# First layer of a two-layer transformer block: VectorE takes two copies from ScalarE in the gelu steps, the rows of maxima are turned ahead of two matmul pairs, and ten filler matmuls become six

## What is computed

```python
xn = _layernorm(x)
x = x + _L0_attn_ref(xn, ...) + _L0_ffn_ref(xn, ...)
xn = _layernorm(x)
x = x + _L1_attn_ref(xn, ...) + _L1_ffn_ref(xn, ...)
```

## Time and profile before

| | |
|---|---|
| median of 3 runs | 1325.0 us |
| lowest and highest | 1321.04 and 1330.04 us |
| the profiled execution's own time | 1330.59 us |
| its span in the profile | 1328.9 us |
| mean granted clock of TensorE | 0.978 |
| first layer | to about 510 us of the span |

### The profile page before, as it was taken

One profiled execution on the slowest core, in us unless ns is written; L12 is line 12 of the kernel. 1 busy time (PEld: TensorE's weight loads), 2 busy tenths in 40 slices (PEclk: granted clock), 3 DMA queues, 4 the chain that ended last, 5 costly groups with the idle time before them and its releaser, 6 DMA issues.

```text
span 1328.9 us, 23542 instructions
## 1 busy us (share of the span) xinstructions
PE 1286.8 (97%) x8338; PEld 773.1 (58%) x8346; DVE 982.7 (74%) x2344; ACT 828.7 (62%) x1235; POOL 744.0 (56%) x889
## 2 busy tenths in 40 slices
PE   8899999999999999999999999999999999999998
PEld 5444445455544445666666666666666666666666
DVE  4666776877776667777777877877877878878775
ACT  2456576666667655666657666666666666656653
POOL 6154465646555445765655655655655665665553
PEclk9889999999999889999999999999999999999999
DMA  6223233424253141111221120020020120010002
GB/s 191 70 75 94 89 99 105 127 91 130 90 165 108 50 142 38 46 41 45 62 66 45 54 74 21 30 74 21 30 74 21 31 74 21 30 50 22 26 30 74
DMA packets 57751, 90.61 MB, mean 68 GB/s; under 512 B 12315, under 2 KB 23616, under 8 KB 57634
## 3 DMA queue, kind: packets, MB, share of 16 engines
q1 hardware_dynamic: 56482, 88.58, 21.4%
q10 hardware_dynamic: 1152, 0.52, 0.1%
HBM read 43.66 MB, written 44.30 MB: 66 GB/s over the span
## 4 chain that ended last, share of the span: by engine, by line
PE 56%; DVE 2%; ACT 2%; POOL 1%; issue 0%; DVEq 0%
PE bank L1674 7%; PE bank_pair L130 6%; PE bank_pair L155 6%; PE bank_pair L1663 4%; PE bank L1663 4%; PE bank L1675 4%; PE bank L1676 4%; PE bank_pair L1664 4%; PE bank_pair L1665 4%; PE bank L1665 4%; PE bank L1664 4%; PE bank_pair L137 1%; DVE bank_pair L165 1%; DVE a_h L1485 1%; DVE a_h L1491 1%; PE bank_pair L1633 1%
## 5 line engine op out<-in xcount | busy, mean ns | idle before, releaser
L1299 POOL TENSOR_TENSOR a_h_lo<-a_h,a_h_hi 128x512 fp32r<-128x512 f32 x256 | 329.8, 1288 | 129.7 <-ACT a_h_hi L1397 125.4
L189 POOL TENSOR_SCALAR_AFFINE_SELECT E<-E 128x256 f32<-128x256 f32 (+1 forms) x384 | 195.5, 512 | 354.0 <-ACT E L1405 199.3
L689 DVE TENSOR_REDUCE mx<-bank_pair 128x2 f32<-128x1024 f32 (+3 forms) x264 | 209.6, 818 | 119.5 <-PE bank_pair L939 118.1
L1485 DVE SCALAR_TENSOR_TENSOR a_h<-a_h,bank_pair 128x512 f32<-128x512 f32 x256 | 175.5, 686 | 122.1 <-ACT a_h L1393 121.4
L1405 ACT ACTIVATE E<-bank_pair 128x1024 f32<-128x1024 f32 (+1 forms) x192 | 169.8, 884 | 116.3 <-PE bank_pair L137 116.3
L165 DVE CUSTOM_DVE_ANT_0 bank_pair<-bank_pair,mask 128x512 f32<-128x512 f32 x496 | 230.3, 516 | 0.0
L1397 ACT ACTIVATE a_h_hi<-a_h 128x512 fp32r<-128x512 f32 x256 | 161.6, 631 | 86.9 <-DVE a_h L1491 86.9
L779 ACT ACTIVATE E<-bank_pair 128x1024 f32<-128x1024 f32 (+1 forms) x192 | 168.4, 878 | 74.2 <-PE bank_pair L137 72.8
L130 PE MATMUL bank_pair<-st 24*128 24x512 f32 (+3 forms) x1024 | 200.2, 390 | 13.4 <-ACT E L779 4.0
L1393 ACT ACTIVATE a_h<-bank_pair 128x512 f32<-128x512 f32 x256 | 152.1, 594 | 73.3 <-PE bank_pair L1665 70.9
L1491 DVE TENSOR_TENSOR a_h<-a_h,bank 128x512 f32<-128x512 f32 x256 | 175.9, 687 | 26.7
(11 more groups left out here) (209 smaller groups left out, 2278.9 us busy)
## 6 DMA issues: line engine op xcount, KB each, us to landing
st<-stack_d SPq DMA_DIRECT2D x256, 96.0 KB
o_d<-O SPq DMA_DIRECT2D x63, 256.0 KB, 2.1
stack_d<-l_q_k_hi SPq DMA_DIRECT2D x56, 256.0 KB, 3.1
stack_d<-l_q_k_lo SPq DMA_DIRECT2D x28, 256.0 KB, 3.4
st<-ms SPq DMA_DIRECT2D x128, 8.0 KB
wst<-wg_in SPq DMA_DIRECT2D x8, 256.0 KB, 3.2
wst<-wu_in SPq DMA_DIRECT2D x8, 256.0 KB, 3.8
wst<-wd_in SPq DMA_DIRECT2D x8, 256.0 KB, 4.4
```

Source lines behind the costliest of these rows:

```text
L189: return nc.gpsimd.affine_select(out=part, in_=part, compare_op=ALU.is_ge, fill=0.0, base=0, pattern=pattern, channel_multiplier=-1)
L689: ins = nc.vector.tensor_reduce(out, pair[:, :, col:col + width(kb)], AX.X, ALU.max)
L1299: nc.gpsimd.tensor_tensor(h_lo[:, q % RH, :], h[:, q % RH, :], h_hi[:, q % RH, :].bitcast(F32), ALU.subtract).then_inc(h_lo_ready, 1)
L1485: nc.vector.scalar_tensor_tensor(hq, hq, 1.0, g_bank[:, :], ALU.add, ALU.mult).then_inc(silu_ready, 1)
```

## The change

In steps with u = 0 that have gelus (b from 0 to 7), and only there: `outputs(g - 1)` and `copy_mrow(g + 1)` move from ScalarE to VectorE, around `add_tile`; `maxima_rows(g + 1)` moves on TensorE from behind `fc(b, 3)` to ahead of `fc(b, 2)`; and the ten fillers of the following step become six.

```diff
-FILLERS = ((2, 2, 2, 2), (10, 2, 2, 0), (2, 2, 4, 3), (2, 2, 2, 3))
+FILLERS = ((2, 2, 2, 2), (6, 2, 2, 0), (2, 2, 4, 3), (2, 2, 2, 3))
...
+            def outputs(g):
+                dve.wait_ge(pv_done, g + 1)
+                if g > 1:
+                    dve.wait_ge(o_out[g % 2], 16 * (g // 2))
+                nc.vector.tensor_copy(O[:, g % 2, :], pv_bank[:, :]).then_inc(O_copied, 1)
+
+            def copy_mrow(g):
+                dve.wait_ge(mT_ready, g + 1)
+                if g > 1:
+                    dve.wait_ge(mrow_in, MAX_LOADS * (g - 1))
+                nc.vector.tensor_copy(ms[:, g % 2, :], bank_of("M", g, 0)[0:MAXIMA, :]).then_inc(mrow_ready, 1)
...
                 if S:
                     negations(g + 1)
+                if u == 0 and ok(b) and in_range(g - 1):
+                    outputs(g - 1)
                 if q is not None:
                     add_tile(q)
+                if u == 0 and ok(b):
+                    copy_mrow(g + 1)
                 if u == 0 and ok(y2) and g < QUADS:
                     statistics(1, y2)
...
-                if in_range(g - 1):
+                if in_range(g - 1) and not (u == 0 and ok(b)):
                     outputs(g - 1)
...
-                if scored(g + 1):
+                if scored(g + 1) and not (u == 0 and ok(b)):
                     copy_mrow(g + 1)
...
                 if u == 0 and ok(b):
+                    maxima_rows(g + 1)
                     fc(b, 2)
                     fc(b, 3)
                 if u == 1 and ok(y2):
                     queries(1, y2)
-                if scored(g + 1):
+                if scored(g + 1) and not (u == 0 and ok(b)):
                     maxima_rows(g + 1)
```

## The result

| | before | changed |
|---|---|---|
| median | 1321.4 us (20 runs) | 1335.5 us (20 runs) |
| lowest, highest | 1318.4, 1330.0 | 1328.4, 1348.0 |
| ratio to before | | 1.0102, interval 1.0084 to 1.0120 |
| profiled execution, span | 1330.6, 1328.9 | 1330.7, 1329.0 |
| mean granted clock of the profiled execution | 0.978 | 0.977 |

What follows compares the result with a forecast made beforehand. Each passage was bound by ScalarE up to the score unit, then by the normalized tiles' chain, starting on VectorE. Path +0.85 and clock +3.2 gave +4.05 us on 1330.6, 1334.6; less 5.6 for the median, 1329 us; range 1318 to 1340.

Steps and rivals of the forecast that it cites:

- rival (a): Every passage from step 9 on loses the clock at step 29's price: +13.1 us, 1338 us; chance 0.17.
- Points 1 to 3: Gelu passages: output copy frees ScalarE 0.60 us, fc 2 and 3 end 0.33 later, maxima copy's leaving saves 0.45.
- Point 5: VectorE ahead of `add_tile`: the output copy, 0.68 us, fits into 1.26 us of idle time and costs nothing.
- Point 6: VectorE behind `add_tile`: the maxima copy takes 0.68 us and makes the statistics, `xn` and transposes 0.63 us late.
- The path terms: Delays and savings in steps 1, 5, 9, 13, 17, 21, 25 and 29, without the clock: together +0.85 us.
- Point 4: TensorE: four fillers, 1.02 us, must go for the 0.45 us and buy nothing beyond; step 1 saves about 1.7.
- Point 7: TensorE ahead of the transposes: 1.64 us more idle time, four more clock falls at 0.8 us, +3.2 us.
- Rival (b): The 8-partition copy takes 0.17 us, `xn` is only 0.12 us late, the clock gains: middle 1321 us; chance 0.25.
- Rival (c): TensorE's order gives ScalarE's gain back, unseen slack takes up the statistics' delay: 0 us, 1325 us; chance 0.08.

Runs made afterwards that it cites:

- the run with the turn alone: Kernel before with only the turn of the maxima (`maxima_rows`) moved ahead of fc 2, ten fillers, both copies on ScalarE: 1322.2 us, ratio 1.0000.

## Why the prediction was right and wrong

The measured 1335.5 us lies in the range (1318 to 1340), and the direction was right. The size was not: +4 us forecast, +14.1 measured, nearer to rival (a), which I gave 0.17. That the time lies inside is in part luck: the range was drawn wide enough to take in rival (a), +13.1 us, and it stood on a median of 1325.0 us from three runs, where twenty give 1321.4. The mechanism was right, a longer wait for the tiles and the clock; the term for the clock was mis-sized by a factor of four, and the fillers' part in it was missing.

- Points 1 to 3, ScalarE: the table load started right behind the exponential, the gelus were bound by TensorE at the back, as said. The gain was 0.58 us rather than 0.45, and as forecast none of it reached the end of the passages 9 to 21. In step 5 all of it did (0.58 for 0.45). Step 1 is shorter, from its first table load to the output copy 16.32 us (48.06 to 64.38) in place of 17.54 (47.27 to 64.81): 1.2 us, where I had 1.7.
- Point 5, the output copy: covered, 0.68 us. Right, and the run with it alone shows no loss clear of noise.
- Point 6, the maxima copy: forecast 0.68 us and 0.63 us of delay; measured 0.68 and 0.64, and 0.60 us a passage in step 9. Right for the passages like it. Two other terms of the sum were off, and cancelled. For steps 13 and 21 I took 0.24 us each, because the tiles had been early there. They were early because the clock was low (0.50 from 226.90 to 230.10 us and from 342.90 to 346.10) and TensorE late; in the run with the turn alone, where the clock was full, it waits 0.40 us in both, and the change costs 0.6. Steps 25 and 29 I read as like step 9, but there TensorE had no idle time ahead of the transposes before the change; step 25 shows 0.18 in place of 0.63. The path terms together come to about +1.0 us, and I had +0.85.
- What the path costs in the times agrees with that only roughly: two runs of the changed kernel and three of the other at the same mean clock of 0.983 differ by some 2.6 us (1328.4 and 1328.5 against 1325.7 to 1326.1). The 1.5 us between the two figures are not settled.
- Point 4 failed in one sentence: that beyond the 0.45 us the removed fillers "buy nothing". Taken out alone they cost 7.4 us. Their worth was the clock, and I counted idle time only for the two edits together, behind the score unit.
- Point 7, the clock, is the mis-sized term. I took four falls at 0.8 us. A fall in these passages costs 3.5 us (20.14 against 16.67). The price of 0.7 us came from setting step 6 against step 10 and taking the wait of 2.10 us off. But step 10 is not step 6 at the full clock. In the profile of the changed kernel with ten fillers step 6 keeps the full clock, through the same wait of 2.10 us, and takes 14.24 us, where it took 18.38:

```profile
125.39:139.63 14.24, 12.10 (x110) 6.37 (x111) 10.30 (x26) 7.93 (x11) 8.01 (x13) 1.00 0.20 69
```

So the loss of the clock costs 4.1 us in step 6 too. Step 29, with 2.45 us, was the nearer row and still low: with the full clock it takes 16.34 us in the run with the turn alone, where it took 18.80. Three falls at 3.5 in place of four at 0.8 make the sum +11.3 us, and a fourth +14.8. The median clocks say the same, as an estimate: 0.975 against 0.989 over 1335 us is 37 us more at half rate (0.014 x 1335 / 0.5), and at 3.5 us for 10 us of it that is 13 us.

- The carry-over from the profiled execution to the median, 5.6 us, was from three runs; with twenty it is 9.2 us. The profiled execution of before had more low clock (0.978) than the median one (0.989 in the runs beside the experiments). Falls counted in its profile, such as in step 29, were no fixed part of the time before, so more of them could be new: that hid a part of the loss.

Rival (b) is out: the copies of 8 and of 128 partitions took 0.68 us each, and the kernel is not faster. Rival (c) is out too.

## What to carry to other kernels

Fillers on TensorE may look surplus where the engine that TensorE waits for ends after them. Here their worth was the granted clock, and it showed in the spread of the executions, while the two profiled ones were equally long. Take the price of a lost clock from the same place at both clock levels, and look at a dozen executions with their clocks, not at one. And when work moves to an engine with idle time, ask which place in its order the idle time is: here 1.3 us lay ahead of `add_tile`, and the copy that was put behind it delayed a chain with no slack.

## What the hardware showed that I had not expected

- Two passages with the same program and the same waits can end differently: in the changed kernel's profile steps 9, 13 and 17 kept 2.4 GHz through waits of 0.77 and 1.6 us, and step 21 did not. With six fillers alone step 9 took 15.93 us and step 13 19.84. Step 6, with one wait of 2.10 us, had a mean clock of 0.72 in the profile of before and 1.00 in that of the changed kernel with ten fillers. What decides it is not shown.
- After such a wait the granted clock stayed at 0.50 for about 10 us (342.90 to 353.00), although TensorE was busy 8.72 of 10.10 us there.
- Matmuls without a result shortened the changed kernel: 36 of them, six in each of six waits, by 8.9 us.
